# Key-weight loads on one queue, the last graph's stores on another, one group's scales moved: a graph-attention kernel on one core

## What is computed

```python
h = jnp.maximum(_layernorm(x, axis=-1), 0.0)
output = h @ weight;  q = h @ wq;  k = h @ wk
alpha = jnp.einsum('bno,bmo->bnm', q, k)
alpha = jnp.maximum(alpha, 0.0) * (graph != 0)
alpha = softmax(alpha, axis=1)
x = x + jnp.einsum('bnm,bmo->bno', alpha, output)
```

## Time and profile before

| | |
|---|---|
| median of three runs | 413.31 us (412.66 to 413.48) |
| the profiled execution | 412.91 us, of which the span shown in the trace is 411.1 us |
| busy in the span: PE / DVE / ACT / POOL | 405.3 / 298.1 / 277.7 / 264.7 us |
| PE's last matmul ends | about 4.1 us before the span's end |
| granted TensorE clock | 1.00 in all 40 slices of the span |
| HBM read, written | 24.12 MB, 16.78 MB |

### The profile page before, as it was taken

How to read it: one execution, slowest core, us unless ns; L and a number is a source line. 1 busy time by engine, 2 the same in 40 slices (tenths; PEclk the granted TensorE clock), 3 DMA queues, 4 the chain that set the end, 5 groups by cost and what they waited for, 6 DMA issues and landing times.

```text
span 411.1 us, 9529 instructions
## 1 busy us (share of the span) xinstructions
PE 405.3 (99%) x3580; PEld 321.7 (78%) x3580; DVE 298.1 (73%) x571; ACT 277.7 (68%) x592; POOL 264.7 (64%) x286
## 2 busy tenths in 40 slices
PE   8999999999999999999999999999999999999995
PEld 5444545979797997979798897979889797979884
DVE  5797789896867676776767777676777667656565
ACT  4749887765867677766777776776867777644534
POOL 0767896979495866759395775939577584910004
PEclk9999999999999999999999999999999999999999
DMA  8973858989889897997969498985978599493022
GB/s 284 373 110 67 217 103 217 232 205 217 181 208 191 245 155 212 189 204 188 192 212 196 156 214 199 197 218 173 198 241 158 156 220 181 75 197 112 2 104 102
DMA packets 161641, 75.03 MB, mean 183 GB/s; under 512 B 135360, under 2 KB 143808, under 8 KB 161600
## 3 DMA queue, kind: packets, MB, share of 16 engines
q1 hardware_dynamic: 161168, 73.81, 77.6%
q10 hardware_dynamic: 432, 0.66, 0.4%
HBM read 24.12 MB, written 16.78 MB: 99 GB/s over the span
## 4 chain that ended last, share of the span: by engine, by line
PE 90%; DVE 4%; DMA 2%; ACT 1%; SPq 1%; issue 1%; POOL 0%; DVEq 0%; POOLq 0%
PE bank L1166 10%; PE bank L1165 10%; PE bank L1163 10%; PE bank L1181 10%; PE bank L1180 10%; PE bank L1178 10%; PE s_bank L1192 3%; PE s_bank L1193 3%; PE s_bank L1194 3%; PE bank L1199 2%; PE bank L1200 2%; PE bank L1201 2%; PE bank L1320 2%; PE bank L1322 2%; PE bank L1321 2%; DMA x_sb<-in_x 2%
## 5 line engine op out<-in xcount | busy, mean ns | idle before, releaser
L423 POOL TENSOR_TENSOR hn_lo<-h,hn_hi 128x512 f16<-128x512 f32 x64 | 74.0, 1166 | 53.1 <-ACT hn_hi L554 52.9
L544 ACT ACTIVATE h<-x_sb,shift,rstd 128x512 f32<-128x512 f32 x64 | 50.0, 804 | 24.0 <-POOL shift L418 23.6
L449 POOL TENSOR_TENSOR hn_lo<-s,hn_hi 128x512 f16<-128x512 f32 x56 | 63.3, 1163 | 0.3 <-ACT hn_hi L559 0.3
L1163 PE MATMUL bank<-hT_hi,mt_hi 128*128 128x256 f16 x224 | 61.1, 273 | 0.0
L1165 PE MATMUL bank<-hT_lo,mt_hi 128*128 128x256 f16 x224 | 61.1, 273 | 0.0
L1180 PE MATMUL bank<-wt_lo,hT_hi 128*128 128x256 f16 x224 | 61.1, 273 | 0.0
L1166 PE MATMUL bank<-hT_hi,mt_lo 128*128 128x256 f16 x224 | 61.1, 273 | 0.0
L1178 PE MATMUL bank<-wt_hi,hT_hi 128*128 128x256 f16 x224 | 61.1, 273 | 0.0
L1181 PE MATMUL bank<-wt_hi,hT_lo 128*128 128x256 f16 x224 | 61.1, 273 | 0.0
L559 ACT ACTIVATE hn_hi<-s 128x512 f16<-128x512 f32 x56 | 33.8, 625 | 25.6 <-POOL s L438 19.9
L1180 PE MATMUL bank<-w_lo,hT_hi 128*128 128x256 f16 x168 | 45.8, 273 | 0.0
(11 more groups left out here) (169 smaller groups left out, 1115.2 us busy)
## 6 DMA issues: line engine op xcount, KB each, us to landing
out_h<-x_sb SPq DMA_DIRECT2D x63, 256.0 KB, 2.1
x_sb<-in_x SPq DMA_DIRECT2D x15, 1024.0 KB, 5.5
adj_sb<-in_adj SPq DMA_DIRECT2D x16, 256.0 KB, 5.3
hn_hi<-in_L_gnn_wq SPq DMA_DIRECT2D x4, 256.0 KB, 5.6
x_sb<-in_x SPq DMA_DIRECT2D x2, 512.0 KB, 7.2
w_sb<-in_L_gnn_weight SPq DMA_DIRECT2D x2, 512.0 KB, 8.7
hn_lo<-in_L_gnn_wk ACTq DMA_DIRECT2D x2, 256.0 KB, 3.8
hn_lo<-in_L_gnn_wk SPq DMA_DIRECT2D x2, 256.0 KB, 3.7
```

Of the source, the lines that this page charges most:

```text
L423: nc.gpsimd.tensor_tensor(hn_lo[:, s, b], h[:, b], hn_hi[:, s, b], ALU.subtract).then_inc(h_split, 1)
L449: nc.gpsimd.tensor_tensor(low, s32[:, f], high, ALU.subtract).then_inc(s_split, 1)
L544: nc.scalar.activation(h[:, b], x_sb[:, s, b], ACT.Relu, bias=shift[:, b:b + 1], scale=rstd[:, b:b + 1]).then_inc(h_made, 1)
L1163: nc.tensor.matmul(o, bh[:, k, cols], ah[:, :, k], start=first and c == 0 and k == 0, stop=False, skip_group_check=True)
```

## The change

1. SP issues all four loads of `wk`, in order, and ACT none.
2. The second half of graph 3 of the last group is stored by ACT, behind the first half, and not by SP. Each store has the wait that it had.
3. On POOL, group 2's layernorm scales come before the sums of M and not between the third and the fourth.

```diff
@@ SP
-            for r in (0, 2):
+            for r in range(K):
                 sp.dma_start(wk_sb[:, r], wk[r * N:(r + 1) * N, :]).then_inc(wk_loaded[r], 16)
@@ SP, end
-            sp.wait_ge(out_read, B)
-            sp.dma_start(out_dram[:, B - 1, HD:], x_sb[:, LAST % UNROLL, GB - 1, HD:]).then_inc(stored[LAST % UNROLL], 16)
@@ POOL
             for b in range(GB):
                 lo_of_h(1, 1, b)
+            layernorm_scales(2)
 
             pool.wait_ge(m_copied, K)
...
             nc.gpsimd.tensor_tensor(mt32[:, T2], m32[:, HK:, HD:], mt32[:, T1], ALU.subtract).then_inc(mt_summed, 1)
-            layernorm_scales(2)
             pool.wait_ge(mt_summed, 3)
@@ ACT, start
-            for r in (1, 3):
-                act.dma_start(wk_sb[:, r], wk[r * N:(r + 1) * N, :]).then_inc(wk_loaded[r], 16)
-
@@ ACT, end
-            act.wait_ge(out_read, B - 1)
-            act.dma_start(out_dram[:, B - 1, :HD], x_sb[:, LAST % UNROLL, GB - 1, :HD]).then_inc(stored[LAST % UNROLL], 16)
+            for f in range(2):
+                act.wait_ge(out_read, B - 1 + f)
+                act.dma_start(out_dram[:, B - 1, HD * f:HD * (f + 1)],
+                              x_sb[:, LAST % UNROLL, GB - 1, HD * f:HD * (f + 1)]).then_inc(stored[LAST % UNROLL], 16)
```

## The result

The changed kernel takes **413.72 us** (median of 15 runs, 413.39 to 414.24); the kernel before took 412.92 beside it (15 runs, 412.53 to 413.49). The ratio is **1.0019, interval 1.0012 to 1.0026**: slower by 0.8 us. Each ratio and its interval come from runs made side by side; they aren't the quotient of the two medians, from which they differ here by up to 0.0017. Its profiled execution took 413.71 us with a span of 411.9, against 412.91 and 411.1. Both profiled executions are typical ones, so the two traces can be laid side by side.

What follows compares the result with a forecast made beforehand. TensorE was taken as the bound, busy 405.3 of 411.1 us. Start -0.3, outputs -0.2, sums of M +0.4 and store -0.1 gave -0.2 us: 412.7 on the profiled 412.91, forecast as 413.1 on the median; range 412.2 to 413.9.

Steps and rivals of the forecast that it cites:

- What bounds it: Whole kernel: TensorE, busy 405.3 of 411.1 us; only its waits or the tail behind its last matmul count.
- The start: Key loads all on SP: x and queries land 0 to 0.65 us sooner; the middle, -0.3 us, was taken.
- the unknown is the hole: Loads, 4.5 to 6 us: 217 GB/s against 385 after; if the two queues cause this dip, 0.65 us is won.
- The bytes ahead of x are the same in both orders: Start: 2.6 MB come before or with x either way, so issuing x at 4.45 instead of 3.55 costs nothing.
- Rival 3: Start: SP's queue alone is slow, from the keys on; x 0.65 us later, +1.25 in all, 414.5 us; chance 0.11.
- The row that I held against it: Loads, 6 to 10 us: SP's queue alone moves 385 GB/s, cited against a slow single queue.
- The sums of M: POOL's sums, moved behind the scales, collide with VectorE's `wt_lo`; TensorE waits at the scores, +0.4 us.
- the played order: POOL's sums and VectorE's `wt_lo` replayed by old durations: low parts of t ready at 45.06, wanted by TensorE at 44.70.
- The bound of 0: M's sums: no loss if the first sum starts after 40.72, when the old alternation with `wt_lo` returns.
- The gap at the outputs: TensorE's 0.2 us gap at 57.93, before group 0's outputs, closes as ACT's exponentials and `p_split` come earlier: -0.2 us.
- The store: Tail: the last half store, issued by ACT 0.15 us sooner, gains -0.1 us; bounds +0.1 to -0.65.
- a used-up cover at the scores: Ahead of `scores(0)`: later low parts of t use up 0.35 us of cover, and TensorE waits until 45.1.

Runs made afterwards that it cites:

- the scales third: Kernel before with only group 2's layernorm scales moved, to between the second and third sum of M on POOL; 412.68 against 412.80 us, ratio 1.0004.
- the loads alone: Kernel before with only the key loads changed, all four of 256 KB issued by SP; 413.45 against 412.80 us, ratio 1.0017.

## Why the prediction went as it did

The time, 413.72, lies in the range, but 413.1 was forecast, a little below before, and the kernel is slower by 0.19%, with an interval that leaves out both no change and a gain. Against the kernel before, -0.2 us was forecast and +0.8 measured; that the time still lies in the range owes something to luck, since the forecast stood on a median of 413.31 and the kernel before took 412.92 beside the changed one. The rival with the mechanism that came, the third, stood at 0.11.

**What bounds it** was right: the four places at which time could be won or lost are those at which the account above finds it, and x's landing passes to the end one for one. (`top_diag`, which isn't among them, decides only with other loads.)

**The start failed: -0.3 forecast, +0.54 measured.** The step that failed is "the unknown is the hole": I took the 217 GB/s of one execution for a property of the order of loads, and let the sum range from 0 to -0.65. Kernels with the same loads show 287 to 339 GB/s in that stretch, and land x at 9.92 to 10.21. So the profiled execution had drawn a start late by 0.1 to 0.4 us, and there was no 0.65 for a change to win. "The bytes ahead of x are the same in both orders" is true and isn't enough: with four 256 KB key loads alone in one queue less was moved from 2 to 6 us than in any other of the kernels in the table, wherever the hole lay, and x is there only when the slowest of 16 DMA engines is done. Rival 3 had that mechanism, the slow stretch beginning with the keys, at 0.11; it had the right place and sign, a price of 0.65 against 0.52, and a reason that is too general, since one queue with the keys in pairs lands x at 9.77 and 10.02 in the fastest executions, and at about 10.35 and 10.5 by the medians. The row that I held against it, 385 GB/s from 6 to 10 us, was of a later stretch and says nothing about the first one.

**The sums of M: +0.4 forecast, +0.44 measured.** First sum undisturbed at 1.27, second and third at 1.73 and 1.72, `wt_lo` at 3.15 together against the 3.14 of the played order (40.72 to 43.86), then the two low parts of t: each step as worked out. The bound of 0, the first sum starting behind the first `wt_lo`, didn't occur; the store and the scales leave that order as it was. The Trainium skill's rule (SBUF — State Buffer, Who interferes with whom), that issue order decides who blocks, agrees with the rows: before, the first `wt_lo` started at 40.72 and the third sum, at 40.88, took 1.72 us; in the change the first sum started first, and the two `wt_lo` took 3.15.

**The gap at the outputs: -0.2, and -0.2.** ACT's 2.0 us wait went, but its exponentials start at 50.43 as before, though `scores(0)` came 0.97 us later. `p_lo` ends at 53.86 + 3.45 = 57.31 instead of 57.87, and TensorE reaches the outputs 0.98 us later: the cover is now over a microsecond. The size was right and the way wasn't: the forecast had the low parts ready sooner because ACT's exponentials come sooner. With the scales third, where TensorE isn't held at the scores, set against the first product with M the exponentials start 0.4 us sooner, but the first `p_lo` only 0.07; the four `p_lo` last 3.44 us instead of 4.34, with less of POOL's work beside them, and that closes the gap. It is read from the rows, not tested by itself.

**The store: -0.1, and 0.** It was issued 0.14 us closer to VectorE's last instruction and took 0.16 us longer to land. That fits a tail set by the bytes of the stores, as the argument went, but no run changed the bytes; the 0.1 was too much.

**Beside the sum:** the first `w_max` at 3.46 and a used-up cover at the scores were as told. The Trainium skill (DMA: Bandwidth & Descriptors, Issuing engines are not separate DMA queues) says that issuing from several engines saves only sequencer time. Here sequencer time was covered (x issued at 4.30 instead of 3.55 lost nothing), and one queue still cost 0.7 us with four loads, and by the medians about 0.3 with two, which the intervals can't tell from nothing: the measurement decides.

What stays open: why four key loads in one queue start more slowly, why some DMA engines fall behind, and why pairs seem better for keys and are bad for queries. The traces show single packets of 0.3 to 1.5 us among ones of 0.08, in the changed kernel 36 of over 0.25 us between 2.2 and 8.4 us and 11 in the kernel before; but in the kernel with all blocks in pairs the last engine lags by over 1 us with 6 such packets. No run separates this further.

## What to carry to other kernels

Where a load has no cover, ask when its last DMA engine is done, and look at several executions before a dip in the transfer rate is taken as something that a change can remove: with the same loads x landed up to 0.4 us apart. The fastest of eleven executions isn't a typical one: two traces here made one queue with pairs look as good as two queues, and the medians don't. Before moving a GpSimd instruction, play VectorE's and GpSimd's instructions against each other by the rows' own durations; that forecast was right to 0.04 us, and it also pointed to a place without the collision, beside small instructions, though the runs can't tell that kernel from the one before. Do it for the tiny instructions as well: one of 3x3 numbers held TensorE up for 0.7 us. An order of loads that lets the first block come sooner is worth nothing if the last one counts.

## What the runs showed of the hardware

- Two queues share the DMA engines about equally: keys and queries on a queue each brought the last key block at 9.3 to 9.6 us instead of 5.5, and two 512 KB loads in one queue land at 4.05 and 5.38, on two queues at 5.36 and 5.73.
- The 16 DMA engines finish one load up to 2.1 us apart (0.4 to 0.8 for x in the good starts), and most of the distance stays for the loads behind it in the queue: with the loads alone 2.12 for the first query block, 1.50 for x.
- With the same loads the start-up rate from 4.5 to 6 us was 217, 287, 321, 322 and 339 GB/s in five kernels.
- A GpSimd subtraction of 128x512 takes 1.27 us alone and 1.72 beside `wt_lo`; small GpSimd instructions of 0.20 us stretch to 0.65 and 0.70; each `wt_lo` takes about 0.7 us, or waits the rest of GpSimd's instruction out. `top_diag`, 3x3 numbers on VectorE, took 1.18 us where it started with a GpSimd subtraction of 1.16.
- The granted TensorE clock fell to 0.50 at 9.1 us, behind a wait of 1.14 us for a load, and was back at 12.5 (kernel with four key singles and query pairs). At the start, transposes follow each other by 0.21 us and later by 0.11; the step lies where the first clock record of the trace stands, at 5.9 us before and at 9.8 to 14 us where TensorE had waited long for keys. The clock of 1.00 in all slices of the page says nothing of the time ahead of that record.
- A 128 KB store issued last took 2.65 us from ACT's queue and 2.5 from SP's; from TensorE's last matmul to the end it came to the same, 4.14 and 4.13.
